# A six-stage decoder on one core: the order of the steps on all five engines is laid out anew

## The reference

```python
x = _layernorm(x + _L0_attn_ref(x, qkv, o_proj, gamma, beta))        # one head, causal, 256 wide
x = _layernorm(x + _L0_xattn_ref(x, k, skip, ctx, ctx, 8))           # long convolution over 128 rows
x = _layernorm(x + _L0_ffn_ref(x, w1, g1, w2, g2, w3, g3))           # ternary weights, 8 bit activations
x = _layernorm(x + _L1_attn_ref(x, Wr, Wk, Wv, Wo, decay, gnw, gnb)) # linear recurrence as a masked product
x = _layernorm(x + _L1_xattn_ref(x, ctx, mask, Wq, bq, Wk, bk, Wv, bv, Wo, qn_w, kn_w)) # 16 heads, 4 of keys
x = _layernorm(x + _L1_ffn_ref(x, w_gating, w_linear))               # gated, products in float8
```

## Time and profile before

| what | value |
|---|---|
| device time, median of 3 runs | 882.16 us (879.91 to 882.3) |
| profiled execution: span from first to last instruction | 880.8 us |
| PE busy | 819.1 us, 93% |
| DVE busy | 694.7 us, 79% |
| ACT busy | 522.0 us, 59% |
| POOL busy | 295.8 us, 34% |
| mean granted clock of TensorE | 0.978 of full speed |

### The profile page before, as it was taken

The page is one execution under the profiler, slowest core; times in us unless marked ns, Lnnn a source line. Parts: engine busy times, 40 slices in busy tenths (PEclk is TensorE's granted clock), DMA queues, the critical chain, the costliest instruction groups (busy, mean ns, idle before and its releaser), DMA issues.

```text
span 880.8 us, 14412 instructions
## 1 busy us (share of the span) xinstructions
PE 819.1 (93%) x5004; PEld 638.4 (72%) x5004; DVE 694.7 (79%) x1703; ACT 522.0 (59%) x1299; POOL 295.8 (34%) x315
## 2 busy tenths in 40 slices
...
GB/s 285 368 143 86 13 37 13 1 25 13 1 1 25 25 13 2 25 13 13 13 1 37 1 13 13 1 37 1 13 1 1 13 0 1 4 11 1 13 1 24
DMA packets 37062, 28.65 MB, mean 33 GB/s; under 512 B 18688, under 2 KB 34560, under 8 KB 36608
## 3 DMA queue, kind: packets, MB, share of 16 engines
...
...
## 4 chain that ended last, share of the span: by engine, by line
PE 63%; DVE 21%; issue 6%; ACT 6%; DMA 1%; POOL 1%; SPq 1%; DVEq 0%; POOLq 0%; ACTq 0%
PE bank L1320 9%; PE bank L1359 8%; PE bank L1047 6%; PE bank L1338 5%; PE bank L1348 5%; PE bank L1238 5%; PE bank L1148 2%; PE bank L1343 2%; PE bank L1118 2%; PE bank L1119 2%; DVE S L975 2%; PE bank L1186 2%; PE bank L1116 2%; PE bank L1041 2%; DVE Zc L789 1%
## 5 line engine op out<-in xcount | busy, mean ns | idle before, releaser
L1320 PE MATMUL bank<-XTE,w_xq 128*128 128x256 f32 x512 | 123.0, 384 | 1.2 <-ACT QA L664 1.2
L672 ACT ACTIVATE S<-S,mx 128x128 f32<-128x128 f32 x256 | 99.4, 394 | 41.0 <-DVE mx L978 40.6
L1359 PE MATMUL bank<-w_xo,OX 128*128 128x256 f32 x512 | 116.0, 380 | 0.0
L1320 PEld LDWEIGHTS bank<-XTE,w_xq 128*128 128x128 f32 x512 | 95.1, 192 | 18.8 <-issue 5.3
L1359 PEld LDWEIGHTS bank<-w_xo,OX 128*128 128x128 f32 x512 | 95.9, 190 | 15.5 <-issue 2.8
L389 POOL TENSOR_TENSOR rq<-vq,minus_half 128x8 f32<-128x8 f32 x32 | 53.3, 1665 | 141.3 <-DVE vq L966 141.3
L663 ACT ACTIVATE QS<-bank,per_partition_sb 128x256 f32<-128x256 f32 x128 | 60.6, 473 | 54.4 <-PE bank L1320 47.7
L975 DVE SCALAR_TENSOR_TENSOR S<-bank,rq,xmask 128x128 f32<-128x128 f32 x256 | 71.7, 343 | 15.5 <-PE bank L1338 10.2
L1338 PEld LDWEIGHTS bank<-KTX,QA 128*128 128x128 f32 x512 | 63.7, 192 | 9.9 <-issue 7.5
L286 POOL TENSOR_TENSOR prod<-XTA,ccolA 128x256 f32<-128x256 f32 x96 | 60.3, 659 | 25.4 <-PE bank L1119 17.3
L1338 PE MATMUL bank<-KTX,QA 128*128 128x128 f32 x512 | 67.9, 277 | 0.2 <-ACT OX L684 0.2
...
## 6 DMA issues: line engine op xcount, KB each, us to landing
...
taps_sb<-in_taps SPq DMA_DIRECT2D x1, 2048.0 KB, 11.3
...
ccolA<-in_ctxT SPq DMA_DIRECT2D x32, 64.0 KB, 2.6
...
w_xq<-in_L_xattn_Wq SPq DMA_DIRECT2D x1, 2048.0 KB, 12.0
w_xo<-in_L_xattn_Wo SPq DMA_DIRECT2D x1, 2048.0 KB, 17.4
...
```

What stands on the lines that cost most here:

```text
L672: ins = nc.scalar.activation(S[:, b, seq(h)], S[:, b, seq(h)], ACT.Exp, bias=mx[:, b, h:h + 1], accum_out=sm[:, b, h:h + 1])
L1320: ins = nc.tensor.matmul(cols(EQ)[:, h], w_xq[:, k, hh * XDIM:(hh + 1) * XDIM], XTE[:, k], start=k == 0, stop=k == HALVES - 1)
L1359: ins = nc.tensor.matmul(rows(EY)[:, b], OX[:, h, b], w_xo[:, n * XGROUP + h], start=n == 0 and h == 0 and b == 0, stop=n == XKV - 1 and h ...
```

## The change

The strings of `ORDER` are replaced. The letters of each string are as many as before and each station keeps its own order, so every engine has the same steps, instructions, buffers and waits, mixed otherwise. Of 711 places in PE's string, 663 in DVE's, 540 in ACT's, 187 in POOL's and 41 in SP's, many hold another letter than before, mostly by a swap of near neighbours; the last eleven letters of PE's string are the same. The diff, cut to the first line of each string (SP's is whole):

```diff
 ORDER = {
     "pe": (
-        "sassasaaasaaaaasaaqaaqasaqqqcqaccaccaqaaccccaaqaaraaraaaraqraqrqqrraacaqcqacqacxyqcqaqaqcaqaaqccaqac"
+        "ssasasaaasaaaasaaaqaaaqasqqqqcaccaccaaqaccccaqaaaraarraaaarqarqrrqaqacaqcqacqcaqcqayqxacqaaqacacaaqa"
...
     "dve": (
-        "aasssassaaasaassaaaasaasasaasaqasaasaasaqaqacacacccccaccacaqaccaacqaaaaaqaaaaaaaaararararararaccrraa"
+        "aasssasasasaassaaaasaaassaaqaaasaaaaaqsaqacacasccccacscaccaqaccaacaaaqaaaqaaaraaraaaaararararacrcrac"
...
     "act": (
-        "sassaasaasassssscqsqqcqacscaacccscaaccccarrrqqqqcaaacqacqacqcccqcaqcqccqycxyyccycxyxxyqxaqyxacaaaqyc"
+        "sassaasaassasssscqqqcsacccaccacqaasccccarrrqcsqqaaqacqacqcqccacqcacqcccqyqyxyccycxyxxyqxqaxayacqaayc"
...
     "pool": (
-        "sassaaaaaaqaqcaccaacaqaaqararcarcaqacaqaaacqcaaccqcaacqaacaaoqcqcqaqcccaqaqcaaaacaaqcaoqcqcqccaqacqa"
+        "sasaasaaaaqaqcaccaacaqaaraqaracrcaacaqaaaqccaqacccqaacaqacoacqaqcqacccqaqaqacaaacqaacaoqcqccqcaqacaa"
...
     "sp": (
-        "asssasqssasaqssaaqaaaaqoaaqoaaqoaaqoqoooo"
+        "sasqsassaassqssaqaaaqaaqoaaaooaqaoqaqoooo"
     ),
```

More of the change, by code:

```diff
@@ L1376 @@
     "pe": (
-        "sassasaaasaaaaasaaqaaqasaqqqcqaccaccaqaaccccaaqaaraaraaaraqraqrqqrraacaqcqacqacxyqcqaqaqcaqaaqccaqac"
-        "ayaaycyccxcyxayxcocqyxaqcxqaaxoaqycaqcyxqxycxaaqoqcayqacqxyaxaxocaccycaqaacqcqacxqcxayqxaqycqacqaycq"
-        "axqyoaaqaacqxcyqxyoaqaaqcayxqyacxyxoacaqaaxqaxaqaycayaxycaccqayoycqccqcyaqcaxcqaxqcqayqaxqyoqyaaxqaa"
-        "xcyqxoqycqaxcyqaqaxcyxaqacoqaxyaqxyaqxacqaaqccaacqxaaqxoqcyaqcccaxqcaqcyaxycqaxyqyaoqcayqaxaaqcoqyxc"
-        "qyaxcyaxcayqyoaqxcayxcqcxcqoqcaacqacaacaqcaacaaxqycxaqyxqyoqaxaxqxcyqacyaxqayoqacaqxqxyaaqcyxqyxoacq"
-        "aaqyaxcqayccycqaxoaqaxqacaxaqycyqcqcaqacyqcaaqcqayoyqyxaqxaqxcqoycxyqycxqaxcoycxyqxyaxqcoqyayqcyxqac"
-        "xcqaaxocqycqcycqyxqcaqcxqxyqycqoxqayxqaxqaoyqyxaqyxqxoyqyaxqyxqaxoqayaxqaxyqxyaqaoxqyaxyaxyaoxyaxaya"
+        "ssasasaaasaaaasaaaqaaaqasqqqqcaccaccaaqaccccaqaaaraarraaaarqarqrrqaqacaqcqacqcaqcqayqxacqaaqacacaaqa"
+        "ycqyacyccxcyxaycxocqyaqxcxqaqaoxaycaqcyxqxycqxaqoacyaqcaayxayxqcocaxcacqaacqcqcaxqxcayqxcaqyqcaqyacq"
+        "aqxyoaaqaayqcxcqyxqaoacaqayxqyacxyxoaqacaaxyaqxayacqxycaqcaacoaycqcycqcayqcaxcqaqxcqayqayxqoqaycxaqa"
+        "axyqxycqoqayxcqaacqxxayqacqoxyaaqxyaqxcaaqacaqcaqacaqxoxcyqacccqxaqcaqcyaxycqaxyqaoyqcaayqxaacqoqxyc"
+        "qyaxycaxacqyoqxayayqxccxccqocqaxcacaxcaqyaacaqacqaacyqaqxqyoxaxqaxcqycayaxqayqoqaxacqaxayycqxyoaqcqx"
+        "aayxqacyqacqcycaxqxaaoqaqcaaqxccycqyaqcayacqaqcqayoyqxayqxaqxcqoycyxqycxaxqcoyacxyqyxqxoycyqaqxycqcx"
+        "cqoayxcqcaccqyqxycqxaqacqxqycyqoxqyqaxaqxoyaqyaqxyxqxoyqyaxqyxqaxoqaayxqaxyqxyaqaoyxaqxyaxayoxyaxaay"
         "aoaaaaaaaaa"
@@ L1392 @@
-        "xaqcaxcaqcoaqaoayqayaaxaaaxqcccaaacaycaacayacacaccqyaxyxcycqaxycxcccyaxyccqoaxqoaayqccqycxaxcqccycac"
-        "yacxcxcqyaxyaxaqyxyoxoaqayaxyxaqaaxyxayqaaxyaxyaaaaaooaaaaaaaaa"
+        "aasssasasasaassaaaasaaassaaqaaasaaaaaqsaqacacasccccacscaccaqaccaacaaaqaaaqaaaraaraaaaararararacrcrac"
+        "accaqacccaaqcacaayaaaaxaayaaacccqaaxyacayccacxaacxayccqccyacxaxacayqxcyaacaxacacacaccqaaoacaaacqcaay"
+        "qaaxqacxacyoacqcxaaccyacxyaccaacaaqaaaxcyayxqcaacyaxyaxaaacaaaaccccqaaayaqaacaaycaacoaqaxoqccxcycacq"
@@ L1394 @@
+        "caycaccxacaxayyaaqxaaaxcycyaqacxaxacccaqaacaqcaaaqayqaxaaacxaayaaccaqaoacocacxcacxcaycycacacaaqyxaya"
+        "xacaacyqcxyacccxcacqaxccxcqayoaqycaacacaqoaaaaaacacaaacaaqacaxcayxccyxaaxayaqacacyaxaxaayacqccycaccx"
+        "qaaqacxaqcyaqycaaaaoaaxacqccaaxaacacayacoayacaacccqyxxycaycxyaxcqcyccyxcacqxoaqyqqcacycxxaccqcycocya"
+        "caxcaxcqyaxyaxaqyxyxqaoayaxyxaqoaaxyxayqaaxyyxaaaaaaooaaaaaaaaa"
     ),
     "act": (
-        "sassaasaasassssscqsqqcqacscaacccscaaccccarrrqqqqcaaacqacqacqcccqcaqcqccqycxyyccycxyxxyqxaqyxacaaaqyc"
@@ new lines @@
+        "xqxcyqxcyaqcxccyqycxcxcccccxqcyxqxayqaxqayqayqaaqcyaaqyxcxcqaxyqaaaqcyxayccxyaxqccyxxqcycccyccyxcyqa"
+        "qaxayqqyaxcaqaqxyqaayxqxyccqxyqaxycaqcacxaaqxcycqxyaxcccyqxcqxcxqccqayqxayxqayqacyqaayxaacqyxqcqxycy"
+        "axccayacxyqacaqycxcxccxcyaxccqqxyqyqxcqxxayqcaxyaqacyxqaayxqcaaqcyxyqcyacxcaqxacayqacccxyxayqqxccxcy"
+        "qyqqyqqycyqxaxqyxcqyycxqacxycaxcycxycqxyqcyaxcayxccaxyqacxcqyacyqxqyqxqyqxqyxqaxaqyxayqyaxxyqxyqyaxa"
+        "xqyaxqaxyyxqaxayqyxaxyaaxyaxayaxyaaaaaaa"
```

11 lines of the change are left out of this document (1 added, 10 removed).

## The result

| | before | after |
|---|---|---|
| device time, median of 4 runs each | 881.03 us (878.55 to 882.3) | 889.29 us (887.92 to 891.32) |
| ratio, with its 95% interval | | 1.0094 (1.0072 to 1.0117) |
| profiled execution, span | 880.8 us | 888.2 us |

The changed kernel is slower by 8.3 us, 0.94%. The forecast was 2.8 us slower, 885.0. The sign and the range (873 to 897) hold, but the size is three times the forecast one. The profiled executions differ by 7.4 us.

What follows compares the result with a forecast made beforehand. TensorE, busy 93% of the span, was taken as the bound, so only its waits could change. Terms -0.8 + 4.8 - 1.2 gave +2.8 us, 883.6 on the profiled span, 885.0 us as the median; range 873 to 897.

Steps and rivals of the forecast that it cites:

- the load of `gate`: SP issues `gate` behind the `b_ot` wait, so ACT's cast waits and both groups' chains come later near 90 us: +4.8 us.
- of this 1.4 to 2.0 us come back: Part of ACT's delay at the first tanh is regained, as the cast of `up` now stands later: 1.4 to 2.0 us.
- the lower clock behind the wait: TensorE products behind the wait for `gate` run at half speed: one or two times 1.9 us, left in the range.
- First 58 us: Two set-up steps cost +1.5 us, `dinv` and `dscaleT` leaving DVE's convolution steps give -2.3: `b_ot` of group 0 0.8 us earlier.
- `K` by `dinv` on POOL: Near 105 us POOL takes `K` first, so L1047 near 124 us gains: -1.2 us, bounds -3 and 0.
- Casts of `up` and `lin`: Both stand later on ACT, their loads in time; about 1 us near 89 us is covered by a parallel chain: zero.
- the first scores: They leave a place near 143 us and fill two idle stretches of about 1 us behind L1320: zero.
- 160 to 840 us: Neighbour swaps in TensorE's busy middle, between gaining its 12.1 us idle and doubling it: zero.
- the middle gets worse: Rival: TensorE's 12.1 us idle double in part, decided by DVE holding a needed step behind a waiting one: +8, 893 us; chance 0.20.
- The test that I named: TensorE should have about 12 us idle from 160 to 840 us; if far from that, the middle's order decides.
- The end: PE's last eleven steps are the same and the 13.5 us idle there stay: zero.

Runs made afterwards that it cites:

- e1_new_start: The changed kernel's order on every engine up to about 164 us, the old order behind it, against the kernel before: 886.3 us, ratio 1.0052.
- the best start: New order to about 164 us with `w_xq`, `w_xo` and `gate` issued ahead of the `b_ot` wait, old order behind, against before: 880.21 us, ratio 0.9976.

## Why the prediction was right and wrong

- **Slower, and by the load of `gate`:** right. The exchange of one pair of steps on SP takes the whole loss away, and L526, L533 and L1066 stall as described. L533 came 7.6 us later than before (75.30 for 67.69), where 6.0 was said. Of that, 6.0 are the late load, and 1.6 are there with the load early too, since the cast of `gate` stands ahead of L533 in the new order.
- **The size of this term, +4.8 us: wrong, it is 8.0.** Two steps of its working failed. First, "of this 1.4 to 2.0 us come back, because before the cast of `up` stood between the first tanh and the second". At the second tanh it did: DVE's first L858 came 7.0 us later than before (76.91 for 69.92), the second 5.9 (78.30 for 72.40). But TensorE takes the next product of this chain, L1186, behind L1066 and L1047, which wait for L533. It started 8.3 us later than before (82.26 for 73.93), the third L858 7.7 us later, and so the gain was lost. The working followed ACT and DVE and left out this order on TensorE. Second, the lower clock behind the wait was named ("one or two times 1.9 us, which I leave in the range") and left out of the sum. It cost 2.4 us. By the prediction's own times TensorE would wait some 4 us there (L1186 done at 70.6, L533 begun at 73.7 and L1066 1.1 behind it, as after), and the earlier trace rows showed what a product costs behind a wait of 3.22. It belonged in the sum. The landing was off by less: 74.3 us for 72.6. At 93 us the kernel is 6.4 us late, where 4.0 was said for 90 us.
- **First 58 us, -0.8: wrong.** `b_ot` of group 0 did come earlier (`cnat` was issued at 52.34 us for 53.53, 52.7 was said), but `UA`, with which the LayerNorm begins, came 1.1 us later in the two profiles. Over all traces `UA` starts at 53.6 to 54.3 us with the old start (three) and at 53.1 to 55.3 with the new first 42 us and `wscale` late (eight), and these overlap: the gain of 0.8 us is not there, and whether it is a loss is not settled. `dinv` was counted as it left the chain, and `wscale`, which came onto it, was not, although the order shown ahead of the prediction has its two rows. At its old length it would have cost 0.3 us; beside POOL's L467 it took 2.0. The start itself cost about 1 us (0.6 to 2.3 by the ratios), where 1.5 was said.
- **`K` by `dinv` on POOL, -1.2:** the sign and, in the whole new order, the size hold (1.2 us at 142 us). That it depends on what DVE has queued behind `K` was not seen. L1047 started 5.2 us later than before (129.17 for 123.97), where 2.8 was said. With the load early it started 2.8 us earlier than before (121.19), so the load's 8.0 are the difference here too.
- **Casts of `up` and `lin`, zero, and the first scores, zero:** the new start without the late load gains 1.5 us from 62 to 93 us and 1.9 us from 142 to 164. Both are gains that the prediction costed at nothing. The first looks like the clock and not like the casts. Four products L1238 that stood ahead of L1083 now stand between L1083 and L1088, and behind them TensorE has the full clock for L1199: it took 1.96 us at 89.14 with the load early, and 3.59 at 89.46 before. From 84 to 94 us the granted clock was 0.86 in place of 0.50. No single edit was tried at either place.
- **160 to 840 us, zero: wrong, +4.3,** within its own bounds of -12 and +12. The reason given for zero, that the swaps on the engines go mostly the same way, did not bring it there, and the bounds were taken from idle time alone. The rival "the middle gets worse" was put at +8 and on DVE. It was half of that, and the longest waits there are for ACT, not for DVE. The test that I named, idle time far from 12 us, missed it: the idle time is 12.97 us, and the loss is in the busy time.
- **The end, zero:** right for the change (34.5 us in place of 34.6 from 846 us on).

In sum the forecast was -0.8 + 4.8 - 1.2 + 0 = +2.8. Measured at equal work it is +8.0 for the load, -4.8 for the rest of the start, +4.3 for the middle and -0.1 for the end, together 7.4.

Two things follow. **The step that failed in the sum is the middle**: put at zero, it cost 4.3 us, and that is nearly all of what separates 2.8 from 7.4. **The start came out right by luck**: it was forecast at +2.8 and measured at +3.2 (+1.8 in `e1_new_start`, with the same start), but of 8.0 and -4.8, where the prediction has 4.8 and -2.0. The load's term was 3.2 us too small and the gains 2.8 too small, and the two errors cancel. That a shift at the start is carried through holds: the best start was 4.9 us early from 265 to 846 us without a change.
